# Score matmuls on 64-row tiles: heads of opposite parity share TensorE, one staged load, the weight splits and some GpSimd jobs move

## Chip, cores and metric

One NeuronCore of a Trainium2 chip. The metric is the device time of one execution in microseconds (us); each time shown is from the chip.

## What is computed

One block of a transformer on x of 4 batches x 512 tokens x 256, with modulation (adaLN), attention and a mixture of experts:

```python
mod = silu(c) @ wmod                      # six rows of 256 per batch: sa, ca, ga, sb, cb, gb
h = layernorm(x) * (1 + ca) + sa
q, k, v = split(h @ Wqkv.T + bqkv)        # 16 heads of 16
scores = q @ k.T * 16 ** -0.5             # causal: k > q becomes -inf
x = x + ga * (softmax(scores) @ v @ Wout.T + bout)
h = layernorm(x) * (1 + cb) + sb
x = x + gb * (shared_expert(h) + top_1_of_8_experts(h))   # silu(gate) * up, then down
```

The weights and activations that are multiplied are held as two 16-bit halves (high and low part), so that a product takes three matmuls.

## The kernel before

**Attention.** The tokens of a batch are four blocks of 128. The 16 heads of a batch form four groups of four heads; a group holds heads of one parity (`group_heads`: groups 0 and 2 even heads, 1 and 3 odd heads). For a pair of heads (even, odd) queries and keys stand one above the other in the stacks `qs` and `ks`, 48 rows (three 16-bit parts of 16 dimensions) from row 0 for the even head and 48 rows from row 64 for the odd one. `ks` holds ones elsewhere. `qs` of before has a copy for each parity with zeros in the other head's rows, so that a matmul over all rows sees one head. The last two rows of `qs` take the negated maxima of the rows, as high and low part.

The scores are computed twice. `scores(N)` (S, L1615) computes queries x keys, and a matmul (L1617) of the constant `maskb` with `identb` adds -1e30 above the diagonal; VectorE reduces the result to row maxima (`maxima`, L1137). `max_turn` transposes the maxima, VectorE negates them, SyncE writes them to `ng_d` (`maxima_out`, L559) and reads them back into `qs` (`maxima`, L566), for half the heads of a batch at a time. `scores_t(n)` (T, L1644) then computes the transposed scores with the maxima subtracted, ScalarE takes the exponential (`exps`, L887), GpSimd zeroes the masked triangle (`mask`, L759) and `values` (L1660, four 128x32 tiles side by side) multiplies with v. `turn_out` (L1670) transposes the result.

**The loop.** A batch is 44 steps, 11 for each group (`UNITS`). At step n of batch b each engine does T number 44 b + n, and S of number 44 b + n + 33 (`LAG`), that is three groups ahead: its heads have the opposite parity. The first 33 score units of batch 0 are computed in the head by another routine, `scores_apart`, on tiles of 32 rows (L1592). T writes two banks in turn (`t_bank`), S three others, so T of a step waits for the exponential of two steps earlier and S for the maximum of three steps earlier.

**Side jobs.** The table `SIDE` puts the other work (projections `qk` and `v`, transposes, output, statistics, modulation, router) at fixed steps; every engine walks the same steps, and `side_jobs(b, n)` gives it its part. On GpSimd `h_low` and `qk_low` (L733, L740) make low parts, `modulate2` (L766, L767) modulates, `bias_x` adds the bias, and `mask` stands at steps 3, 7, 9 and 10 of a group.

**Weights.** 27 pieces of the experts' weights are loaded (`stage_load` on SyncE for the first three, afterwards from ScalarE's queue), and split into halves during attention. `SPLITS` says at which step of which batch ScalarE makes the high half of piece k (`split_high`, L937); VectorE makes the low half two steps later (`LOWS`, L1238), and four steps later (`MOVES`) ScalarE waits for it and issues the write of the halves and the load of piece k + 3.

**The queue of SyncE** is written out by hand. In the head it issues for batches 0 and 1, for each half f of the heads, the writes of queries and keys to memory (`qk_out`, L532, six transfers), their reads into the stacks (`stacks`, L549, four), the maxima, the modulation rows (`mod_rows`, L555) and the first three staged loads. A wait in it holds up all that follows.

## Time and profile before

| what | us |
|---|---|
| runs shown: median, lowest, highest | 470.62, 469.96, 471.55 |
| the profiled execution | 467.88 |
| its span | 466.1 |
| TensorE busy | 401.6 (86%) |
| VectorE busy | 313.4 (67%) |
| ScalarE busy | 228.0 (49%) |
| GpSimd busy | 211.4 (45%) |
| mean granted clock of TensorE | 0.969 |

The span runs from the first to the last instruction that the profiler saw. PE is TensorE's matmuls, PEld its weight loads, DVE VectorE, ACT ScalarE, POOL GpSimd, SP SyncE; a q behind a name means the queue's sequencer, which waits or issues transfers. The ends of matmuls are modelled, so busy time of PE includes the way through the array. A granted clock of 1.00 is 2.4 GHz, 0.50 is 1.2 GHz.

### The profile page before, as it was taken

Reading aid. Unit: us, or ns where it says so; the run is one execution under the profiler, and the core shown is the slowest. Engines: PE = TensorE matmul, PEld = TensorE weight load, DVE = VectorE, ACT = ScalarE, POOL = GpSimd, SP = SyncE. Lnnn points to the kernel's source line nnn. Section 1 sums busy time; section 2 is a strip of 40 time slices with the busy share of each in tenths; the row PEclk is TensorE's granted clock in tenths of the full one; section 3 lists DMA queues with packets and bytes.
Section 4 is the critical chain, followed back from the end, with each engine's and each line's share of the span. In section 5 each row is a group of like instructions: output and inputs, shape, how many; then the busy total and the mean of one; then the engine's idle time right before and its main releaser. Section 6 shows DMA issues by size and latency. Waiting matters only on the chain.

```text
span 466.1 us, 8603 instructions
## 1 busy us (share of the span) xinstructions
PE 401.6 (86%) x3009; PEld 226.4 (49%) x3009; DVE 313.4 (67%) x635; ACT 228.0 (49%) x408; POOL 211.4 (45%) x251
## 2 busy tenths in 40 slices
PE   3789984889879879878988878999998999999991
PEld 3244532334544446433544345565655666666660
DVE  7678594359888878998887853789844444444441
ACT  2445663577574757736777545345222323232320
POOL 2395952543227934368252862110510646464332
PEclk9999998699999999997999979999999999999997
DMA  8456489268942588945446201995531454434210
GB/s 269 159 131 143 164 237 227 91 184 212 257 112 90 175 190 261 288 133 169 128 137 213 62 1 46 344 358 202 148 123 46 73 96 72 89 65 87 27 20 0
DMA packets 46192, 67.96 MB, mean 146 GB/s; under 512 B 5380, under 2 KB 33668, under 8 KB 46152
## 3 DMA queue, kind: packets, MB, share of 16 engines
q1 hardware_dynamic: 31064, 36.74, 27.8%
q10 hardware_dynamic: 9936, 22.55, 14.8%
q0 software_dynamic: 5152, 8.14, 8.9%
q8 instruction: 26, 0.43, 0.4%
q14 instruction: 14, 0.11, 0.1%
HBM read 43.14 MB, written 25.18 MB: 147 GB/s over the span
## 4 chain that ended last, share of the span: by engine, by line
PE 57%; DVE 16%; ACT 6%; POOL 6%; DMA 5%; issue 5%; SPq 3%; ACTq 1%; DVEq 0%; POOLq 0%
PE bank L1504 35%; PE bank L1660 5%; PE bank L1644 4%; DVE mx L1137 3%; PE bank L1615 3%; DMA stage<-in_down 2%; PE bank L1885 2%; DMA qk_d<-W 2%; ACT W L887 2%; PE bank L1592 1%; SPq L532 1%; DVE x_sb L1182 1%; DVE rowg L1238 1%; POOL W L740 1%; POOL W L759 1%
## 5 line engine op out<-in xcount | busy, mean ns | idle before, releaser
L887 ACT ACTIVATE W<-bank 128x512 f32<-128x512 f32 (+1 forms) x176 | 93.8, 562 | 63.5 <-PE bank L1644 42.4
L1137 DVE TENSOR_REDUCE mx<-bank 128x1 f32<-128x384 f32 (+3 forms) x176 | 105.2, 633 | 26.2 <-PE bank L1617 22.5
L1504 PE MATMUL bank<-W 128*128 128x256 f16 (+2 forms) x756 | 104.7, 291 | 4.5 <-DVE x_sb L1182 1.8
L1504 PEld LDWEIGHTS bank<-W 128*128 128x128 f16 x756 | 73.0, 99 | 37.8 <-issue 8.2
L759 POOL TENSOR_SCALAR_AFFINE_SELECT W<-W 128x512 f32<-128x512 f32 x64 | 48.7, 764 | 86.9 <-ACT W L887 86.8
L1644 PE MATMUL bank<-W 128*128 128x512 f16 (+3 forms) x256 | 64.1, 308 | 20.1 <-ACT W L887 18.8
L1504 PE MATMUL bank<-W,h2T 128*128 x276 | 67.3, 380 | 0.8 <-issue 0.8
L830 POOL DMA_INDIRECT out<-h2T,sidx x23 | 36.3, 1578 | 64.1 <-DVE h2T L1474 63.8
L1615 PE MATMUL bank<-W 126*128 126x128 f16 (+3 forms) x208 | 53.6, 309 | 5.2 <-DVE mx L1137 4.7
L1660 PE MATMUL bank<-W 128*32 128x128 f32 (+3 forms) x512 | 49.6, 462 | 4.5 <-POOL W L759 4.4
L1644 PEld LDWEIGHTS bank<-W 128*128 128x128 f16 x256 | 21.5, 98 | 58.5 <-ACT W L887 36.7
L1504 PE MATMUL bank<-h2T,W 128*128 128x512 f16 x192 | 43.1, 379 | 0.6 <-DVE W L1253 0.6
L1467 DVE TENSOR_TENSOR W<-bank,W 128x512 f16<-128x512 f32 x23 | 15.9, 692 | 37.4 <-ACT W L1048 37.4
L1048 ACT ACTIVATE W<-bank 128x512 f16<-128x512 f32 x23 | 13.7, 597 | 55.1 <-PE bank L1885 55.1
L1504 PEld LDWEIGHTS bank<-W,h2T 128*128 128x128 f16 x276 | 26.3, 97 | 26.3 <-issue 5.1
L816 POOL DMA_INDIRECT rowg<-h_d,gidx x23 | 23.6, 1028 | 31.4 <-DVE gidx L1417 24.7
L1617 PE MATMUL bank<-maskb,identb 128*128 128x128 bf16 (+2 forms) x143 | 35.7, 250 | 0.0
L1504 PEld LDWEIGHTS bank<-h2T,W 128*128 128x128 f16 x192 | 18.5, 98 | 21.9 <-DVE W L1253 1.0
L1238 DVE SCALAR_TENSOR_TENSOR rowg<-stage,rowg 128x1024 f16<-128x1024 f32 x18 | 23.3, 1293 | 7.6 <-ACT rowg L937 7.6
L876 ACT ACTIVATE W<-bank,bqk 128x512 f16<-128x512 f32 (+1 forms) x32 | 20.3, 685 | 15.8 <-PE bank L1504 15.6
L1615 PEld LDWEIGHTS bank<-W 126*128 126x128 f16 x208 | 19.5, 99 | 15.5 <-DVE mx L1137 7.7
L1269 DVE TENSOR_TENSOR h2T<-bank,h2T 128x256 f16<-128x256 f32 x23 | 9.8, 425 | 21.9 <-ACT h2T L916 21.9
(173 smaller groups left out, 557.3 us busy)
## 6 DMA issues: line engine op xcount, KB each, us to landing
w_d<-rowg ACTq DMA_DIRECT2D x18, 512.0 KB, 3.8
W<-w_d SPq DMA_DIRECT2D x18, 512.0 KB, 8.0
stage<-in_gup ACTq DMA_DIRECT2D x14, 512.0 KB
qk_d<-W SPq DMA_DIRECT2D x48, 128.0 KB
W<-qk_d SPq DMA_DIRECT2D x32, 192.0 KB, 5.5
stage<-in_down ACTq DMA_DIRECT2D x7, 512.0 KB
x_sb<-in_x SPq DMA_DIRECT2D x4, 512.0 KB, 8.9
h_d<-gbb SPq DMA_DIRECT2D x4, 512.0 KB, 4.6
```

Of the source, the lines that this page charges most:

```text
L759: g.affine_select(out=d, in_=d, compare_op=ALU.is_ge, fill=0.0, base=0, pattern=[[0, 4], [1, P]], channel_multiplier=-1).then_inc(s_msk, 1)
L816: g.indirect_dma_start(rowg[:, r % RG, :], None, h2_d, bass.IndirectOffsetOnAxis(ap=gidx[:, r:r + 1].bitcast(U32), axis=0)).then_inc(s_gr[ ...
L830: g.indirect_dma_start(out.rearrange("b s n -> (b s) n"), bass.IndirectOffsetOnAxis(ap=sidx[:, r:r + 1].bitcast(U32), axis=0), ry[r % YR], ...
L876: a.activation(dst, side_bank("qk", b, u)[:, :], ACT.Identity, bias=bqk[:, 2 * isk + u // 2:2 * isk + u // 2 + 1], scale=1.0 / WS if isk e ...
L887: a.activation(PT[j][:, i:i + m, :], t_bank(N)[:, 0:m * w].rearrange("p (i n) -> p i n", i=m), ACT.Exp).then_inc(s_exp, 1)
L1137: v.tensor_reduce(mx_v[:, b % 2, hp0 // 4, par, i:i + m, t], s_bank(N)[:, 0:m * w].rearrange("p (i n) -> p i n", i=m), AX.X, ALU.max).then ...
L1238: v.scalar_tensor_tensor(split_part(k, 1), staged(k), WS, split_part(k, 0), ALU.mult, ALU.subtract).then_inc(s_el, 1)
L1504: i = t_.matmul(outp, l, r, start=(n == 0), stop=(n == len(prods) - 1), **kw)
L1615: t_.matmul(bk[:, w * i:w * (i + 1)], qs[r][0:P - 2, hp, par, P * t:w], ks[r][0:P - 2, hp, 0:w], start=(i == 0), stop=False, skip_group_ch ...
L1617: t_.matmul(bk[:, 0:m * w].rearrange("p (i n) -> p i n", i=m)[:, :, w - P:w], identb[:, :], maskb[:, :].unsqueeze(1).to_broadcast([P, m, P ...
L1644: q = t_.matmul(t_bank(N)[:, w * i:w * (i + 1)], ks[r][:, hp, P * j:P * (j + 1)], qs[r][:, hp, par, P * j:S], start=True, stop=True)
L1660: q = t_.matmul(OTb[32 * i:32 * i + 32, P * j:S], v1[b % 2][:, c:c + 32], PT[j][:, i], start=(j == 0), stop=(j == TT - 1), tile_position=( ...
```

## The change

- **Tiles.** S and T use only the 64 rows of their head (48 rows of scores from row 0 or 64; T two more with the maxima). The maxima go to rows 48 and 49 of each half in place of rows 126 and 127, `qs` has one copy for both parities, and its two memsets of zeros (one on VectorE at the very start, one on GpSimd) go.
- **Mask.** The mask is added by two matmuls over the 64 rows of the same half, each for 64 of the 128 key columns, with new constants `half_q` and `half_m`, which GpSimd makes in the head (`half_constants`). TensorE waits for them once, before the first S.
- **Order in a group.** In steps 8 to 10 of a group T stands behind S.
- **Staged load.** `stage_load(2)` moves on SyncE from behind `mod_rows(0)` to behind `stacks(1, 0)`.
- **Splits.** `SPLITS` has 8, 6, 6 and 7 pieces in batches 0 to 3 in place of 6, 6, 8 and 7, at other steps.
- **GpSimd's jobs.** All but the two statistics and the bias stand two steps later in GpSimd's own order; the masks stay.

```diff
-          0: {6: 0, 12: 1, 18: 2, 25: 3, 32: 4, 39: 5},
-          1: {2: 6, 9: 7, 16: 8, 23: 9, 30: 10, 37: 11},
-          2: {1: 12, 6: 13, 11: 14, 16: 15, 21: 16, 26: 17, 31: 18, 36: 19},
+          0: {6: 0, 12: 1, 18: 2, 23: 3, 28: 4, 33: 5, 38: 6, 43: 7},
+          1: {5: 8, 12: 9, 19: 10, 26: 11, 33: 12, 40: 13},
+          2: {3: 14, 10: 15, 17: 16, 24: 17, 31: 18, 38: 19},
...
+def gpsimd_jobs(b, n):
+
+    if b < 0:
+        return side_jobs(b, n)
+    prompt = ("stats1", "stats2", "bias")
+    return ([j for j in side_jobs(b, n - 2) if j[0] not in prompt]
+            + [j for j in side_jobs(b, n) if j[0] in prompt])
...
+        half_q = sb("half_q", [P, 2, P], BF16)
+        half_m = sb("half_m", [P, P // 2], BF16)
...
-            qs.append(early(NH * S, F16).rearrange("p (h two n) -> p h two n", two=2, n=S))
+            qs.append(early(NH // 2 * S, F16).rearrange("p (h n) -> p h n", n=S))
+            at[0] += NH // 2 * S
...
-                    for a, dst in ((0, qs[r][:, :, par]), (1, ks[r])):
+                    for a, dst in ((0, qs[r]), (1, ks[r])):
...
-                    sp.dma_start(qs[r][P - 2:P, 4 * f:4 * f + 4, par], src[par]).then_inc(s_ng[r][f], 16)
+                    p0 = 64 * par + 3 * HD
+                    sp.dma_start(qs[r][p0:p0 + 2, 4 * f:4 * f + 4], src[par]).then_inc(s_ng[r][f], 16)
...
             stacks(1, 0)
+            stage_load(2)
             qk_out(1, 1)
             stacks(1, 1)
             sp.wait_ge(s_md, 16)
             mod_rows(0)
-            stage_load(2)
...
-                g.memset(qs[1].rearrange("p h two n -> p (h two n)").bitcast(F32), 0.0).then_inc(s_const, 1)
+                g.memset(ones16[:, :], 1.0).then_inc(s_const, 1)
                 po.wait_ge(s_const, 4)
-                g.memset(ones16[:, :], 1.0)
...
+            def half_constants():
+
+                link(g.memset(half_q[:, :, :], 0.0))
+                for lo in (0, P // 2):
+                    rows = slice(lo, lo + P // 2)
+                    link(g.memset(half_m[rows, :], 0.0))
+                    link(g.affine_select(out=half_m[rows, :], in_=half_m[rows, :], compare_op=ALU.is_ge, fill=NEG,
+                                         base=0, pattern=[[-1, P // 2]], channel_multiplier=1))
+                    link(g.affine_select(out=half_m[rows, :], in_=half_m[rows, :], compare_op=ALU.not_equal, fill=NEG,
+                                         base=-(P // 2 - 1), pattern=[[0, P // 2]], channel_multiplier=1))
+                    for part, half in ((0, 0), (1, 0), (1, 1)):
+                        sel = half_q[rows, part, 64 * half:64 * half + 64]
+                        link(g.affine_select(out=sel, in_=sel, compare_op=ALU.not_equal, fill=1.0,
+                                             base=0, pattern=[[-1, P // 2]], channel_multiplier=1))
+                    for part, half, value in ((0, 0, 0.0), (1, 0, 1.0), (1, 1, 0.0)):
+                        sel = half_q[rows, part, 64 * half:64 * half + 64]
+                        link(g.affine_select(out=sel, in_=sel, compare_op=ALU.not_equal, fill=value,
+                                             base=-(P // 2 - 1), pattern=[[0, P // 2]], channel_multiplier=1))
+                g.tensor_copy(ve1[0:1, 0:1], ve1[0:1, 0:1]).then_inc(s_half, 1)
+                po.wait_ge(s_half, 1)
...
-                    for job, c, k in side_jobs(b, n):
+                    for job, c, k in gpsimd_jobs(b, n):
...
-            v.memset(qs[0].rearrange("p h two n -> p (h two n)").bitcast(F32), 0.0)
...
+                if N == LAG:
+                    pe.wait_ge(s_half, 1)
...
-                    t_.matmul(bk[:, w * i:w * (i + 1)], qs[r][0:P - 2, hp, par, P * t:w],
-                              ks[r][0:P - 2, hp, 0:w], start=(i == 0), stop=False, skip_group_check=True)
-                t_.matmul(bk[:, 0:m * w].rearrange("p (i n) -> p i n", i=m)[:, :, w - P:w], identb[:, :],
-                          maskb[:, :].unsqueeze(1).to_broadcast([P, m, P]), start=False, stop=True,
-                          skip_group_check=True).then_inc(s_s1, 1)
+                    p0 = 64 * par
+                    t_.matmul(bk[:, w * i:w * (i + 1)], qs[r][p0:p0 + 3 * HD, hp, P * t:w],
+                              ks[r][p0:p0 + 3 * HD, hp, 0:w], start=(i == 0), stop=False, skip_group_check=True)
+                rows = slice(64 * par, 64 * par + 64)
+                for part in range(2):
+                    c = w - P + 64 * part
+                    q = t_.matmul(bk[:, 0:m * w].rearrange("p (i n) -> p i n", i=m)[:, :, c:c + 64],
+                                  half_q[rows, part, :], half_m[rows, :].unsqueeze(1).to_broadcast([64, m, 64]),
+                                  start=False, stop=(part == 1), skip_group_check=True)
+                q.then_inc(s_s1, 1)
...
-                    q = t_.matmul(t_bank(N)[:, w * i:w * (i + 1)], ks[r][:, hp, P * j:P * (j + 1)],
-                                  qs[r][:, hp, par, P * j:S], start=True, stop=True)
+                    rows = slice(64 * par, 64 * par + 3 * HD + 2)
+                    q = t_.matmul(t_bank(N)[:, w * i:w * (i + 1)], ks[r][rows, hp, P * j:P * (j + 1)],
+                                  qs[r][rows, hp, P * j:S], start=True, stop=True)
...
-                    if b >= 0:
+                    if b >= 0 and n % UNITS < 8:
...
+                    if b >= 0 and n % UNITS >= 8:
+                        scores_t(BU * b + n)
```

TensorE, batch 0, steps 7 to 9 of its second group, before (L1644 is T, L1615 S, L1617 the mask, L1660 `values`):

```order
L1615 MATMUL bank<-W 128x512
L1617 MATMUL bank<-maskb,identb 128x128
L1644 MATMUL bank<-W 128x256 x2
L1615 MATMUL bank<-W 128x512
L1617 MATMUL bank<-maskb,identb 128x128
L1660 MATMUL bank<-W 32x512 x4
L1644 MATMUL bank<-W 128x256 x2
L1615 MATMUL bank<-W 128x512
L1617 MATMUL bank<-maskb,identb 128x128
```

and after (L1683 is T, L1649 S, L1654 the mask's two matmuls, L1699 `values`):

```order
L1649 MATMUL bank<-W 128x512
L1654 MATMUL bank<-half_m,half_q 128x64 x2
L1649 MATMUL bank<-W 128x512
L1654 MATMUL bank<-half_m,half_q 128x64 x2
L1683 MATMUL bank<-W 128x256 x2
L1699 MATMUL bank<-W 32x512 x4
L1649 MATMUL bank<-W 128x512
L1654 MATMUL bank<-half_m,half_q 128x64 x2
L1683 MATMUL bank<-W 128x256 x2
L1649 MATMUL bank<-W 128x512
```

From step 8 on T has moved behind S and the mask, and stands next to `values`; the mask is two matmuls.

SyncE, in the head, from the stacks of batch 1's first half, before (L549 `stacks`, L532 `qk_out`, L555 `mod_rows`, L501 the staged load, L559 and L566 the maxima of batch 0's second half):

```order
L549 DMA W<-qk_d 48x4x512 x4
L532 DMA qk_d<-W 8x16x512 x6
L549 DMA W<-qk_d 48x4x512 x4
L555 DMA W<-mod_d 128x768
L501 DMA stage<-in_down 128x4x256
L559 DMA ng_d<-negm 32x2x128
L566 DMA W<-ng_d 2x4x512 x2
```

and after (L559 `stacks`, L514 the staged load, L545 `qk_out`, L565 `mod_rows`, L569 and L577 the maxima):

```order
L559 DMA W<-qk_d 48x4x512 x4
L514 DMA stage<-in_down 128x4x256
L545 DMA qk_d<-W 8x16x512 x6
L559 DMA W<-qk_d 48x4x512 x4
L565 DMA W<-mod_d 128x768
L569 DMA ng_d<-negm 32x2x128
L577 DMA W<-ng_d 2x2048 x2
```

The staged load has moved ahead of six writes, four reads and the modulation rows.

ScalarE, batch 2, around step 22, before (L887 exponentials of steps 21 to 26, L937 the high half of a split, L941, L494 and L495 its move and the load behind it):

```order
L887 ACTIVATE W<-bank 128x512
L937 ACTIVATE rowg<-stage 128x1024
L887 ACTIVATE W<-bank 128x512 x4
L941 DMA w_d<-rowg 128x2048
L494 DMA stage<-in_sgw 128x512
L495 DMA stage<-in_suw 128x512
L887 ACTIVATE W<-bank 128x384
```

and after (L919 exponentials, L969 high half, L973, L507 and L508 move and load, L927 the copy that was L895):

```order
L969 ACTIVATE rowg<-stage 128x1024
L919 ACTIVATE W<-bank 128x384
L919 ACTIVATE W<-bank 128x512 x3
L973 DMA w_d<-rowg 128x2048
L507 DMA stage<-in_sgw 128x512
L508 DMA stage<-in_suw 128x512
L919 ACTIVATE W<-bank 128x512 x3
L969 ACTIVATE rowg<-stage 128x1024
L919 ACTIVATE W<-bank 128x512
L919 ACTIVATE W<-bank 128x384
```

Before, the split of step 21 is moved four exponentials later, at step 25. After, the splits stand at steps 17 and 24 and the first one's move at step 21.

## Rows read from the trace of the kernel before

**Rows 1.** Busy time of the engines by stretch: length, then each engine; clock, transfers.

```profile
53.80:86.30 32.50, 21.77 (x165) 10.96 (x165) 22.06 (x47) 17.14 (x31) 15.94 (x19) 0.88 0.71 187
86.30:114.90 28.60, 25.86 (x190) 11.85 (x189) 18.48 (x32) 19.56 (x35) 12.43 (x17) 0.95 0.66 182
114.90:175.80 60.90, 51.32 (x437) 27.29 (x436) 51.64 (x104) 39.06 (x71) 30.70 (x39) 1.00 0.61 168
175.80:230.10 54.30, 48.00 (x410) 25.07 (x408) 49.22 (x96) 34.76 (x62) 28.19 (x38) 0.94 0.68 207
230.10:288.60 58.50, 50.40 (x395) 25.57 (x394) 41.83 (x77) 36.92 (x68) 28.34 (x35) 0.94 0.30 92
70.00:80.00 10.00, 4.85 (x37) 2.58 (x35) 5.24 (x10) 4.10 (x8) 2.91 (x3) 0.94 1.05 258
```

**Rows 2.** Chain that ended last, shares by line, windows 86:115, 115:176, 176:230.

```profile
by line: PE bank L1660 18.9%; PE bank L1504 18.9%; PE bank L1644 17.3%; PE bank L1615 14.1%; PE bank L1617 6.7%; PE bank L1670 4.0%; DVE rowg L1238 3.9%; ACT rowg L937 3.3%; ACT W L887 3.1%; issue 3.0%; ACT W L876 2.4%; ACTq L499 1.6%; ACTq
by line: DVE mx L1137 7.5%; POOL W L740 7.4%; PE bank L1504 7.0%; DVE rowg L1238 6.2%; POOL rowg L766 6.2%; issue 5.8%; POOL W L759 5.6%; POOL rowg L767 5.1%; DVE x_sb L1182 4.1%; PE bank L1660 3.8%; ACT W L887 3.7%; ACTq L501 3.4%; PE bank
by line: PE bank L1660 15.8%; PE bank L1644 14.2%; PE bank L1504 11.4%; PE bank L1615 10.2%; issue 6.3%; ACT W L887 5.0%; DVE x_sb L1182 4.6%; PE bank L1617 4.1%; ACT rowg L937 3.0%; DVE rowg L1180 2.9%; DVE st L1187 2.4%; PE bank L1670 2.4
```

**Rows 3.** Timeline of SyncE's queue: start, us, engine, line, transfer.

```profile
59.62 3.66 SPq L532 DMA_DIRECT2D qk_d<-W  x6
...
70.65 0.47 SPq L501 DMA_DIRECT2D stage<-in_down  x1
71.16 0.48 SPq L559 DMA_DIRECT2D ng_d<-negm  x1
82.28 0.55 SPq L566 DMA_DIRECT2D W<-ng_d  x2
```

**Rows 4.** Timeline, ScalarE and TensorE, the stall; idle before in brackets.

```profile
81.57 1.06 ACT L937 ACTIVATE rowg<-stage 128x1024 f16<-128x1024 f32 x1 [7.12 <-DMA stage<-in_down]
...
83.17 0.61 PE L1644 MATMUL bank<-W 128*128 128x128 f16 x4 [7.99 <-ACT W L887]
```

**Rows 5.** Timeline of TensorE in the head: 32-row tiles, whole-array matmuls.

```profile
41.92 0.82 PE L1592 MATMUL bank<-W 32*128 32x512 f16 x12
...
42.80 1.46 PE L1504 MATMUL bank<-W 128*128 128x512 f16 x6
...
49.80 2.76 PE L1504 MATMUL bank<-W 128*128 128x512 f16 x12
```

**Rows 6.** Timeline of TensorE: what follows a mask matmul of 128 columns.

```profile
40.61 0.23 PE L1585 MATMUL bank<-maskb,identb 128*128 128x128 bf16 x1
...
40.77 0.34 PE L1592 MATMUL bank<-W 32*128 32x128 f16 x3
...
60.41 0.22 PE L1617 MATMUL bank<-maskb,identb 128*128 128x128 bf16 x1
...
60.55 1.06 PE L1660 MATMUL bank<-W 128*32 128x512 f32 x8
...
62.00 0.22 PE L1617 MATMUL bank<-maskb,identb 128*128 128x128 bf16 x1
...
62.06 0.38 PE L1644 MATMUL bank<-W 128*128 128x128 f16 x4
```

**Rows 7.** Timeline, VectorE's and GpSimd's memsets, GpSimd's idle time in the head.

```profile
1.71 3.47 DVE L1304 MEMSET W<- 128x4096 f32 x1 [1.71 <-PEq L1942]
...
29.77 3.51 POOL L683 MEMSET W<- 128x4096 f32 x1
...
40.17 1.15 POOL L733 TENSOR_TENSOR W<-W 128x512 f16<-128x512 f32 x1 [4.24 <-ACT W L862]
```

**Rows 8.** Timeline of TensorE in batch 1: `values` behind a mask.

```profile
165.59 0.42 PE L1660 MATMUL bank<-W 128*32 128x128 f32 x8 [1.36 <-POOL W L759]
```

**Rows 9.** Timeline in batch 2: VectorE's half of a split, ScalarE idle.

```profile
207.35 1.22 DVE L1238 SCALAR_TENSOR_TENSOR rowg<-stage,rowg 128x1024 f16<-128x1024 f32 x1
...
210.35 0.49 ACT L887 ACTIVATE W<-bank 128x384 f32<-128x384 f32 x1 [4.91 <-issue]
```

More of the change, by code:

```diff
@@ L317, in build @@
         s_col = sem("s_col")
-        s_zero = sem("s_zero")
+        s_ones = sem("s_ones")
+        s_half = sem("s_half")
         s_mp = sem("s_mp")
@@ L537, in stacks @@
                 sp.wait_ge(s_qkw[r][f], 16 * 6 * (b // 2 + 1))
-                if b == 0 and f == 0:
-                    sp.wait_ge(s_zero, 1)
-                if b == 1 and f == 0:
-                    sp.wait_ge(s_const, 4)
-                    sp.wait_ge(s_zero, 2)
+                if b < 2 and f == 0:
+                    sp.wait_ge(s_ones, b + 1)
                 if b >= 2:
@@ L787, in _ @@
                         more_constants()
+                        half_constants()
                     if b < 0 and n in (25, 38):
@@ L1307, in _ @@
             norm1(0)
-            v.memset(ks[0].rearrange("p h n -> p (h n)").bitcast(F32), ONES).then_inc(s_zero, 1)
+            v.memset(ks[0].rearrange("p h n -> p (h n)").bitcast(F32), ONES).then_inc(s_ones, 1)
             modulation_columns()
             low_qkv()
-            v.memset(ks[1].rearrange("p h n -> p (h n)").bitcast(F32), ONES).then_inc(s_zero, 1)
+            v.memset(ks[1].rearrange("p h n -> p (h n)").bitcast(F32), ONES).then_inc(s_ones, 1)
             stats1(1)
```

## The prediction

> **What bounds the kernel now.** I read the page first, then the busy time of each stage, then the chain of waits, and last the timeline at the places where the chain changes engine. The attention loop (52 to 289 us) is cut by batch, batch 0 again at 86.3 us [rows 1]. TensorE is busy for 25.9 of 28.6 us late in batch 0, 51.3 of 60.9 in batch 1, 48.0 of 54.3 in batch 2; VectorE for 51.6 and 49.2 us in batches 1 and 2. So no engine alone sets the pace. The chain of waits says who does where [rows 2]. Late in batch 0 the two score passes and the mask (L1644, L1615, L1617) hold 38.1% of 29 us, 11.0 us; in batch 2 28.5% of 54 us, 15.4 us; in batch 1 they are not among the first names and GpSimd's lines (L740, L766, L759, L767) hold 24.3% of 61 us. After 289 us the kernel is not touched.
>
> **Early batch 0, a long stall.** SyncE issues the third staged load at 70.65 us, behind both parts of batch 1's stacks [rows 3]. ScalarE reaches the weight split that reads it, gets it at 81.57, and TensorE, two exponentials behind, starts again at 83.17 after 8.0 us idle [rows 4]. That idle time also costs clock: 0.88 of full speed granted over this stage [rows 1].
>
> **What the change costs and saves, on TensorE.** A matmul of 512 columns takes 0.217 us of TensorE: twelve in 2.76 against six in 1.46 [rows 5]. On 32-row tiles, in the same place, twelve take 0.82: four run side by side [rows 5]. A group of 11 steps has 5120 columns in each score pass and 2048 in the mask, 12288 or 5.2 us. In the new order T (`scores_t`) and S (`scores`) of a step read opposite halves of the array and write different banks, so for steps 0 to 7 a step costs the longer of both: 5 x 512 + 3 x 384 = 3712 columns. In steps 8 to 10, S comes first; T of step 9 runs beside S of step 10, T of 8 and 10 are alone because `values` follows: 5 x 512. With the mask's 2048, which the 64-column halves do not change (4 x 64 twice is 4 x 128), 8320 columns are left, 3.5 us; if the second mask half runs beside the next T, some 0.3 less. I take 1.8 us saved per group, 35%. There are 13 such groups (143 units of S): 23 us of TensorE's time.
>
> Against this, every change of tile shape costs. Same shape: the mask at 62.00 is followed at 62.06. Other shape: mask at 60.41, `values` at 60.55; mask at 40.61, 32-row tiles at 40.77 [rows 6]. That is 0.09 to 0.10 us more. Counted in the two orders of instructions, the loop has 132 changes of shape before and 226 after (by batch 29, 34, 34, 35, then 48, 62, 54, 62), because each projection, transpose or shared matmul now stands between 64-row tiles. 94 x 0.095 = 8.9 us. If TensorE had to run empty at each, a switch would cost what a 128-column matmul lasts beyond its columns, 0.22 - 0.055 = 0.165 us, and 94 of them 15.5 us; the rows show the smaller price. The Trainium skill ("TensorEngine Tiling (Array Packing)", Key Properties) has a rule that speaks against the change: a change of the tiling mode, not of the tile, drains the engine; by it the second sum would stand, by the rows the first, and I take the first.
>
> **By stage, on the path.**
> - Head: VectorE's memset of `qs[0]`, 3.47 us, opens the chain [rows 7]. It goes, but the input's landing and TensorE's first matmuls, which wait for the modulation weights, are close behind: -0.4 (0 to -1.5). GpSimd loses a memset of 3.51 us and gets 19 small linked operations and a copy, at 0.25 to 0.36 us each some 5 to 7 us; it has 4.24 us idle before 40.17 [rows 7], so 4.24 + 3.51 covers it. Without that cover it would be late by up to 1 us: then batch 1's low parts and modulation rows, and SyncE's stacks behind them, are late.
> - Early batch 0: the load is now issued at about 59.6 us, before `qk_out(1, 1)`, 11 us earlier, and lands before 71. The 8.0 us don't come back whole. Next late is step 22, which needs the maxima of the second half of the heads: written from 71.16, read back from 82.28 [rows 3]. The transfer engines are busy all of the time from 70 to 80 us, share 1.05 [rows 1], and they drain in order of issue; the bytes ahead of that write are the same, only earlier. `qk_out(1, 1)` is issued 0.5 us later and lands up to 2 us later, the stacks behind it too. I let the maxima land 1 to 3.5 us earlier: -2.5 (0 to -8).
> - Late batch 0: 35% of 11.0 is -3.9; nine or ten switches, four fifths on the path, +0.7; two more splits (a copy of 1.06 us on ScalarE [rows 4] and a pass of 1.22 on VectorE [rows 9] each), some of it in idle time, +1.5. Sum -1.7.
> - Batch 1: T, S and mask on the path, perhaps 3 us: -1.0. GpSimd: its masks are queued behind modulation and low-part jobs; TensorE waits 1.36 us for one at 165.59 [rows 8]. Two steps later for the jobs puts those masks ahead of about 2.7 us of work: -1.9. One more VectorE split spilling in: +0.5. Sum -2.4 (+1 to -7; VectorE's 51.6 + 1.2 us are the floor).
> - Batch 2: 35% of 15.4 is -5.4, switches 20 x 0.095 x 0.6 = +1.2. Two splits fewer, -1. And ScalarE sits idle for 4.91 us before 210.35, stuck at the move of the split of step 21: VectorE's half of it is queued behind the second statistics and starts at 207.35 [rows 9], the exponentials wait behind the move, clock 0.94 in the stage [rows 1]. The splits move to steps 17 and 24, away from step 22: -2 to -4. Together -7 to -9, but VectorE's 49.2 - 2.5 = 46.7 us leave at most 7.6: I take -6.
> - Batch 3: one group has S left (-1.8), 27 more switches +2.6; two fifths on the path: +0.3.
>
> Sum: -0.4 - 2.5 - 1.7 - 2.4 - 6.0 + 0.3 = -12.7. The profiled execution took 467.88 us, the median of the runs is 470.62, 2.7 above; 470.6 - 12.7 = 457.9.
>
> **Rivals.**
> 1. *VectorE, GpSimd and the maxima end it.* The time that TensorE saves turns into waits for VectorE, as in batch 1, where TensorE holds little of the chain [rows 2]. Then stages give 0, -1, -0.5, -1, -2.5: -5, 465.6 us. For: busy shares of 85% and 91%. Against: 15.4 us of plain score matmuls on the path of batch 2.
> 2. *Slower: no overlap.* If T and S don't run side by side (each waits for another engine's semaphore before it, and a waiting T holds up the S behind it), nothing of the 23 us comes, and the switches remain: 8.9 us, of which at the path's shares about 5.5; with mask halves that no longer hide, +1. The stall, the stats collision and the memset return some 5 to 6. That is +1; with each switch at 0.165 us (94 x 0.165 x 0.6 = 9.3 in place of 5.5) +5, 475. This second price is what the skill's rule above would give. The rival decides as soon as fewer than about a quarter of the pairs overlap. Against it: the 32-row tiles of this trace do overlap [rows 5].
> 3. *Clock.* Three times in the loop TensorE fell to 1.2 GHz after waits (shares 0.88, 0.95, 0.94, 0.94 [rows 1]); each time cost some 7 to 10 us at half speed. A TensorE with less to do may fall more often; two more drops of 7 us cost +7: about 465.
> 4. *More.* The stall comes back whole and VectorE closes up: -20, 450.
> 5. *The parts hardly act:* overlap and switches cancel, the stall only moves: within 0.3% (1.4 us, about what a measurement of this kernel can tell from no change).
>
> **How the numbers follow.** Forecast 0.60, with its own range 453 to 463.5; rivals 1 and 3 together 0.20; slower 0.08; more 0.07; none 0.05. Leaving out the slow end and a part of "more" and "none" gives 450 to 467.5. Faster by over 0.3%: 0.60 + 0.07 + 0.20 = 0.87; within: 0.05; slower: 0.08.
>
> **What would show it.** Right: in the timeline T and S starting within 0.01 us of each other; late batch 0 and batch 2 shorter by 2 and 6 us; no idle time of 8 us before 84 but one of some 5 to 6 us at step 22, ended by a transfer; shape changes still 0.15 us from a 128-column matmul. Wrong: S starting 0.2 us behind T; new stretches at 1.2 GHz; GpSimd busy without a break up to 41 us with SyncE's mod rows late; VectorE busy over 95% in batch 1.

## The result, and the profile after

The changed kernel took 476.27 us (median of 4, 470.52 to 477.04), beside it the kernel before 470.29: ratio 1.0097, 95% interval 1.0052 to 1.0141. Later, on another chip, it took 472.41 against 469.80, ratio 1.0030 (0.9990 to 1.0070). So it is 0.3 to 1% slower by the two measurements, and the second can't be told from no change; I had said 458. (A ratio leaves out executions more than 1.5% above their kernel's fastest; a median takes all.)

Busy time by stretch in the profiled execution (476.57 us, span 474.8), cut at the same exponentials as [rows 1], columns as there; the last row is the part behind the loop:

```profile
53.80:86.90 33.10, 21.82 (x188) 11.93 (x189) 22.99 (x47) 17.33 (x31) 17.19 (x20) 0.77 0.72 185
86.90:118.50 31.60, 27.30 (x210) 11.11 (x206) 19.49 (x32) 21.52 (x38) 11.84 (x16) 0.81 0.74 216
118.50:176.60 58.10, 49.72 (x485) 26.00 (x482) 50.33 (x104) 39.34 (x70) 31.99 (x40) 0.94 0.63 178
176.60:233.10 56.50, 48.19 (x451) 24.73 (x449) 48.28 (x93) 31.83 (x59) 26.46 (x36) 0.85 0.54 160
233.10:292.10 59.00, 54.12 (x409) 25.40 (x409) 43.05 (x80) 37.36 (x69) 28.97 (x36) 0.91 0.32 99
292.10:474.70 182.60, 165.38 (x1114) 105.71 (x1106) 91.43 (x205) 56.22 (x107) 63.20 (x53) 0.98 0.42 112
```

Against [rows 1]: +0.6, +3.0, -2.8, +2.2, +0.5 us. The eighth column tells most: the granted clock is lower in every stretch of the loop, 0.77, 0.81, 0.94, 0.85, 0.91 where it was 0.88, 0.95, 1.00, 0.94, 0.94. TensorE's busy time over the five stretches rose from 197.4 to 201.2 us although its matmuls overlap, as more of them ran at half speed. In the loop of this execution TensorE stood at 1.2 GHz ten times, 61 us together; before, three times and 24 us. Counting time at 1.2 GHz as 2 x (1 - clock) x time, it is 69 us of a whole execution in the mean of the four; before, at a mean clock of 0.967, 31 us.

The overlap itself is there. Timeline of TensorE in the kernel after: start, us, line, tile:

```profile
180.21 0.33 PE L1683 MATMUL bank<-W 50*128 50x384 f16 x1
180.21 0.33 PE L1649 MATMUL bank<-W 48*128 48x384 f16 x1
180.38 0.22 PE L1654 MATMUL bank<-half_m,half_q 64*128 64x64 bf16 x2
180.53 0.68 PE L1535 MATMUL bank<-W 128*128 128x256 f16 x4
```

T (L1683) and S (L1649) start together (3 or 4 ns apart in most records where T is issued first, 10 ns in most where S is), and the mask follows 0.17 us later, the time of one pass. By an estimate that sums what each matmul's columns occupy at 2.4 GHz, a group of 11 steps went from 9.5, 11.5, 11.0, 8.3 us (first, sixth, ninth, thirteenth group) to 7.2, 9.7, 9.2, 6.5: 1.8 to 2.3 us, the 1.8 of the forecast. In the records the next shape starts 0.12 us behind the last mask half, which has 64 columns (0.03 us), so a change of shape costs 0.09 as in [rows 6].

Early batch 0 with its stall came out no shorter. SyncE's queue, then TensorE, in the kernel after:

```profile
60.76 0.48 SPq L514 DMA_DIRECT2D stage<-in_down  x1
61.28 4.37 SPq L545 DMA_DIRECT2D qk_d<-W  x6
73.59 2.03 SPq L559 DMA_DIRECT2D W<-qk_d  x4
...
76.15 0.43 SPq L569 DMA_DIRECT2D ng_d<-negm  x1
84.39 0.53 SPq L577 DMA_DIRECT2D W<-ng_d  x2
```

```profile
65.90 0.50 PE L1649 MATMUL bank<-W 48*128 48x128 f16 x3 [2.31 <-DMA W<-qk_d]
...
86.30 0.60 PE L1683 MATMUL bank<-W 50*128 50x512 f16 x1 [6.53 <-DMA W<-ng_d]
```

The chain of waits from 86 to 119 us, in which TensorE's score and mask lines held 38.1% before [rows 2], is now led by the transfers:

```profile
by line: DMA ng_d<-negm 21.5%; DMA qk_d<-W 16.6%; DMA W<-ng_d 15.9%; SPq L545 11.1%; PE bank L1535 8.1%; issue 6.3%; SPq L559 4.6%; PE bank L1699 4.1%; PE bank L1649 3.4%; ACT rowg L969 3.2%; ACT W L908 3.0%; PE bank L1683 2.6%; PE bank L16
```

The load stands 10 us earlier (60.76), but `qk_out(1, 1)` behind it took until 73.59 to land, so the stacks are issued 5.8 us later than before (67.82), the maxima are written at 76.15 instead of 71.16, and their read is issued at 84.39 instead of 82.28 [rows 3]. The 8.0 us of [rows 4] became 6.53, ended by the maxima, and the wait for batch 1's stacks grew from 0.5 to 2.31 us. The load's move also explains the chain from 86 to 119 us: e1 below, which has the move and whole-array tiles, is led there by the same transfers (22.6%, 18.2% and 13.2% of 86 to 116 us), and e7, which has not, by TensorE's lines.

### The profile page after: what moved, and what is told of

It reads as the page before. It is cut to its first block, busy times and chain, and to the rows that moved or that the text cites. A ratio compares the mean times of both kernels' runs of the same rounds, so it can differ in the third digit from the quotient of the medians.

```text
span 474.8 us, 8919 instructions
## 1 busy us (share of the span) xinstructions
PE 407.1 (86%) x3152; PEld 225.9 (48%) x3152; DVE 311.3 (66%) x634; ACT 227.9 (48%) x408; POOL 212.9 (45%) x270
## 4 chain that ended last, share of the span: by engine, by line
PE 53%; DVE 15%; DMA 11%; ACT 7%; issue 5%; SPq 4%; POOL 4%; ACTq 1%; DVEq 0%; POOLq 0%
PE bank L1535 35%; DMA ng_d<-negm 4%; DMA qk_d<-W 4%; DVE mx L1169 4%; PE bank L1699 4%; PE bank L1683 2%; SPq L545 2%; PE bank L1926 2%; DVE rowg L1270 2%; ACT W L919 2%; PE bank L1623 1%; DMA stage<-in_wmod 1%; POOL W L790 1%; PE bank L1649 1%; PE bank L1550 1%
## 5 line engine op out<-in xcount | busy, mean ns | idle before, releaser
L919 ACT ACTIVATE W<-bank 128x512 f32<-128x512 f32 (+1 forms) x176 | 93.6, 562 | 72.0 <-PE bank L1683 49.8
L1535 PE MATMUL bank<-W 128*128 128x256 f16 (+2 forms) x756 | 109.2, 298 | 6.7 <-DVE x_sb L1214 2.9
L1535 PEld LDWEIGHTS bank<-W 128*128 128x128 f16 x756 | 73.9, 101 | 42.6 <-issue 11.6
L1683 PE MATMUL bank<-W 50*128 50x512 f16 (+3 forms) x256 | 65.1, 330 | 19.1 <-ACT W L919 9.9
L1535 PE MATMUL bank<-W,h2T 128*128 x276 | 68.6, 386 | 3.2 <-DVE W L1285 2.0
L1649 PE MATMUL bank<-W 48*128 48x128 f16 (+3 forms) x208 | 57.0, 336 | 8.9 <-DVE mx L1169 6.5
L1699 PE MATMUL bank<-W 128*32 128x128 f32 (+3 forms) x512 | 54.3, 501 | 0.7 <-POOL W L790 0.7
L1683 PEld LDWEIGHTS bank<-W 50*128 50x128 f16 x256 | 18.5, 96 | 53.2 <-ACT W L919 23.1
L1080 ACT ACTIVATE W<-bank 128x512 f16<-128x512 f32 x23 | 13.7, 597 | 55.6 <-PE bank L1926 53.2
L1498 DVE TENSOR_TENSOR W<-bank,W 128x512 f16<-128x512 f32 x23 | 15.9, 692 | 37.4 <-ACT W L1080 37.4
L1654 PE MATMUL bank<-half_m,half_q 64*128 64x64 bf16 (+2 forms) x286 | 38.5, 217 | 0.0
L1654 PEld LDWEIGHTS bank<-half_m,half_q 64*128 64x128 bf16 x286 | 28.8, 105 | 12.3 <-issue 4.6
L1649 PEld LDWEIGHTS bank<-W 48*128 48x128 f16 x208 | 17.0, 99 | 28.5 <-DVE mx L1169 16.1
```

Of the source, the lines that this page charges most:

```text
L919: a.activation(PT[j][:, i:i + m, :], t_bank(N)[:, 0:m * w].rearrange("p (i n) -> p i n", i=m), ACT.Exp).then_inc(s_exp, 1)
L1498: v.tensor_tensor(rhT[:, r % 2, 1].rearrange("p f n -> p (f n)"), T1[:, :], rhT[:, r % 2, 0].rearrange("p f n -> p (f n)"), ALU.subtract). ...
L1535: i = t_.matmul(outp, l, r, start=(n == 0), stop=(n == len(prods) - 1), **kw)
L1649: t_.matmul(bk[:, w * i:w * (i + 1)], qs[r][p0:p0 + 3 * HD, hp, P * t:w], ks[r][p0:p0 + 3 * HD, hp, 0:w], start=(i == 0), stop=False, skip ...
L1654: q = t_.matmul(bk[:, 0:m * w].rearrange("p (i n) -> p i n", i=m)[:, :, c:c + 64], half_q[rows, part, :], half_m[rows, :].unsqueeze(1).to_ ...
L1683: q = t_.matmul(t_bank(N)[:, w * i:w * (i + 1)], ks[r][rows, hp, P * j:P * (j + 1)], qs[r][rows, hp, P * j:S], start=True, stop=True)
```

## The experiments

Sixteen kernels, four at a time, each four on one chip with the kernel before. The clock is the mean over a kernel's executions; before had 0.967 to 0.969 each time.

| kernel | median us | before | ratio (95%) | clock |
|---|---|---|---|---|
| e1 three moves, tiles as before | 462.14 | 467.29 | 0.9893 (0.9840-0.9947) | 0.977 |
| e2 tiles only | 473.71 | 467.29 | 1.0118 (1.0062-1.0175) | 0.926 |
| e3 changed, load back | 469.70 | 467.29 | 1.0021 (0.9983-1.0060) | 0.930 |
| e4 changed, T twice in even steps | 472.10 | 467.29 | 1.0073 (1.0035-1.0111) | 0.939 |
| e5 changed + 64 filler matmuls | 473.96 | 467.30 | 1.0147 (1.0093-1.0200) | 0.945 |
| e6 e1 + the same filler | 465.71 | 467.30 | 0.9984 (0.9949-1.0019) | 0.982 |
| e7 splits and GpSimd, load as before | 459.67 | 467.30 | 0.9852 (0.9807-0.9898) | 0.976 |
| e8 e1, load behind the maxima | 459.98 | 467.30 | 0.9851 (0.9807-0.9894) | 0.977 |
| e9 changed, T and S in one half | 500.68 | 467.12 | 1.072 (of medians; its shortest execution, 487.40, 1.043) | 0.871 |
| e10 changed, transfers as e8 | 467.84 | 467.12 | 1.0009 (0.9977-1.0040) | 0.927 |
| e11 GpSimd's jobs only | 467.87 | 467.12 | 1.0025 (0.9991-1.0059) | 0.972 |
| e12 changed, T first | 469.73 | 467.12 | 1.0013 (0.9976-1.0050) | 0.928 |
| e13 splits only | 468.80 | 469.80 | 0.9952 (0.9924-0.9980) | 0.974 |
| e14 e7, score matmuls on 66 rows | 474.05 | 469.80 | 0.9930 (0.9890-0.9969) | 0.943 |
| e15 e10, T first | 470.66 | 469.80 | 1.0018 (0.9987-1.0049) | 0.928 |
| e16 changed, again | 472.41 | 469.80 | 1.0030 (0.9990-1.0070) | 0.929 |

**Tiles or moves (e1, e2, e3).** Two theories stood against each other: "clock" (the tiles lower it) and "load" (the moved load holds up the transfers behind it). e1 is before with the new table, `gpsimd_jobs` and this; e2 is the reverse, the changed kernel with the three as before; e3 undoes this line alone:

```diff
             stacks(1, 0)
+            stage_load(2)
             qk_out(1, 1)
             stacks(1, 1)
...
             mod_rows(0)
-            stage_load(2)
```

> The kernel before, with only the three moves of the change: the third staged load ahead of qk_out(1, 1), the new table of splits, GpSimd's jobs two steps later. The score tiles stay whole-array. Theory 'load': the moved load holds up what is issued behind it, so batch 1's stacks land later (TensorE waits about 2 us for them near 66 us instead of 0.47), the maxima of step 22 are written out at about 76 us instead of 71.16, and the stall before 86 us stays; the GpSimd wait of 4.4 us shrinks; sum 0 to +3 us against before, 470 to 473. Theory 'clock': the moves have little to do with the loss, the time at 1.2 GHz stays near the 31 us of before, and the kernel stands within 2 us of before. My forecast of record would have had the moves alone at -5 to -7, 464.

> The changed kernel with the staged load, the table of splits and GpSimd's jobs as before, so only the 64-row tiles, the halved mask and the step order are new. Theory 'clock': TensorE has less to do, falls to 1.2 GHz more often (60 us or more at that level against 31), and the saving of the overlap is lost: 468 to 476. Theory 'load': the loss of the changed kernel sits in the moved load, so the tiles alone bring what the forecast gave them (batches 0, 1 and 2: about -8 us): 461 to 464, with the clock of before.

> The changed kernel with the third staged load back behind mod_rows(0). Theory 'load': the stacks land by 64 to 66 us, the maxima are written out at 71 us, batch 1's first exponential starts 3 us earlier than in the changed kernel, and one or two stretches at 1.2 GHz before 130 us go with the waits: 3 to 6 us faster than the changed kernel, 471 to 473. Theory 'clock': the drops after 150 us stay as they are, and it gains at most 2 us: 474 to 476.

The moves alone gain 5.2 us, the tiles alone lose 6.4 (medians), at a clock of 0.926: the loss is the tiles'. In e1 the maxima were written at 74.27 us and the stall was 7.76 us, so the theory on the load was right in its mechanism; but e1 is faster all the same, which neither theory had, and which is the splits' and GpSimd's doing (e7). e3, with the load back, stands at 1.0021, against 1.0097 in the first measurement of the changed kernel, which seemed to bear out the theory on the load; but the changed kernel run again stands at 1.0030 (e16). With the tiles in place, undoing this move brings nothing that shows. e3's twelve executions differ among themselves: 464.58 us at a clock of 0.939, 473.90 at 0.918. A straight line through them gives 0.47 us for each us at 1.2 GHz; through the 23 executions of before beside them 0.59. The Trainium skill ("TensorE: Matmul & The Clock Gate", Terms, `throttle_active_nc0_time_ns`) prices throttled time at a half at this ratio; these two slopes lie on either side of it. The same line through each of the sixteen kernels gives anything from 0.22 to 0.68, 0.43 in the mean, so a half is a fair first price here and no more.

**Does more work raise the clock? (e4, e5, e6)**

```diff
-                for i in range(m):
+                for i in [i for i in range(m) for _ in range(2 - N % 2)]:
```

```diff
+                if N % UNITS in (0, 2, 4, 7):
+                    t_.matmul(t_bank(N)[:, 0:4 * P], identb[:, :], maskb[:, :].unsqueeze(1).to_broadcast([P, 4, P]),
+                              start=True, stop=True)
```

> The changed kernel with the matmuls of T issued twice in every even step (the second writes the same values again): 88 steps, about 41,000 more columns of 64-row tiles, 17 us of TensorE at 2.4 GHz, which brings its score work near that of the kernel before. Theory 'clock': the fuller TensorE falls to 1.2 GHz less often, the time there shrinks from 70 us by a third or more, and the kernel is no more than 4 us slower than the changed one, perhaps faster. If the clock doesn't follow TensorE's load, two thirds of the 17 us are on the path: +10 us or more, 486.

> The changed kernel with one useless whole-array matmul of 512 columns (0.217 us) ahead of T in 4 steps of each group of 11, 64 in all, where TensorE changes its tile shape anyway; T then overwrites what it wrote. 14 us more of TensorE, and some 5 us for 48 more changes of shape. Theory 'clock' (TensorE's level follows how much of the array is at work, and the tiles lowered that): the mean granted clock rises from 0.93 towards the 0.97 of the kernel before, and the time stays within 3 us of the changed kernel or falls below it. If the level doesn't answer to it, 19 us more on TensorE give +8 to +12 us, 482 or more, at 0.93.

> The same 64 useless matmuls at the same places in the kernel with whole-array score tiles and the three moves (the first experiment, 462.1 us, clock 0.978). Here the clock has little left to give, so this shows the plain price of that work: 14 us of TensorE and few changes of shape, about half of it on the path: +5 to +9 us, 467 to 471, by both theories. If it costs as much as in the changed kernel, the clock gave nothing back there.

T twice lifted the clock from 0.929 to 0.939, from 67 us at 1.2 GHz to 58, not by the third that I expected; whole-array filler of fewer columns lifted it to 0.945, 52 us. In time neither gave anything back that shows: e4 (1.0073) is level with the changed kernel (1.0030 and 1.0097), e5 (1.0147) is 0.5 to 1.2% slower, and the same filler in whole-array tiles cost 0.9% (0.9893 to 0.9984), less than the 5 to 9 us that I expected. The clock moves with TensorE's load, but too little to say what it answers to.

**Busy time or rows at work (e9, e14).** e9 moves T to the rows of the other parity: the same matmuls, waits and shapes, no overlap. e14 leaves tiles alone: in e7's kernel both passes read 66 rows of operands, still whole-array matmuls in the same order (the diff shows S; T gets the same `0:66`). Both change the values as well: e9's T computes the scores of the wrong heads, and e14 leaves out nearly all of the odd heads' scores and all maxima.

```diff
-                    rows = slice(64 * par, 64 * par + 3 * HD + 2)
+                    rows = slice(64 * (1 - par), 64 * (1 - par) + 3 * HD + 2)
```

```diff
-                    t_.matmul(bk[:, w * i:w * (i + 1)], qs[r][0:P - 2, hp, par, P * t:w],
-                              ks[r][0:P - 2, hp, 0:w], start=(i == 0), stop=False, skip_group_check=True)
+                    t_.matmul(bk[:, w * i:w * (i + 1)], qs[r][0:66, hp, par, P * t:w],
+                              ks[r][0:66, hp, 0:w], start=(i == 0), stop=False, skip_group_check=True)
```

> The changed kernel, but T reads the rows of the other parity, so T and S of a step use the same half of the array and can't run side by side. T then computes the scores of the wrong heads: this part of the output is not the reference's, the work and its waits are the same. It takes back the whole 23 us of TensorE that the overlap saves and keeps every change of shape. If the clock follows how much of the time TensorE is busy, the mean granted clock goes from 0.927 back to 0.95 or more, and the time moves by -2 to +5 us against the changed kernel (474 to 481). If the clock follows how much of the array is at work (one half at a time here, as little as can be), it stays at 0.93 or falls, and the kernel is 10 us or more slower, 486.

> The seventh experiment's kernel (whole-array score tiles, 459.7 us, clock 0.976), but both score passes read 66 rows of operands in place of 126 and 128, so the matmuls, their columns, their order and their tile shape stay the same and only fewer rows of the array are at work. Half of the heads' scores and the maxima that stand in the other rows are left out of the sums, so the output is not the reference's. If the granted clock follows the rows at work, it falls with no tile or order changed: to 0.95 or less, and the time rises by some 0.5 us for each microsecond at 1.2 GHz, to 464 to 470. If the clock fell in the changed kernel because of idle time, waits or shape changes, it stays at 0.975 and 460.

In e9 the clock fell to 0.871: 129 us at 1.2 GHz. The profiled execution is the longest of the six (503.67 us, clock 0.859); the shortest, 487.40 us, had 0.899, still below every execution of the changed kernel. The first row shows a stretch of e9; the other two show T and S at another place at 1.2 GHz, 0.43 us apart and no longer together:

```profile
227.00:281.60 54.60, 54.32 (x291) 23.53 (x292) 34.03 (x58) 24.91 (x44) 17.94 (x25) 0.50 0.23 76
```

```profile
190.87 0.63 PE L1683 MATMUL bank<-W 50*128 50x512 f16 x1
191.30 0.52 PE L1649 MATMUL bank<-W 48*128 48x384 f16 x1
```

TensorE was busy for 54.32 of 54.60 us and got 0.50 of full speed all that time. So it isn't idle time that keeps the clock down here. The fall itself came behind idle time: in the 5 us before 227.0 TensorE was busy for 3.02. The Trainium skill ("TensorE: Matmul & The Clock Gate", Part 1: The HAM clock gate) has the clock set by how busy the engine has been; this stretch, busy throughout and at 1.2 GHz, differs from that, and the measurement decides. e14 lowers the clock without tiles, more changes of shape or a new order. Batch 2 of e14 in windows:

```profile
174.10:208.60 34.50, 30.12 (x261) 16.69 (x258) 30.16 (x62) 21.16 (x39) 14.61 (x23) 1.00 0.74 205
208.60:229.10 20.50, 19.71 (x94) 9.11 (x94) 13.61 (x25) 9.66 (x17) 9.01 (x13) 0.50 0.31 98
```

and the same windows of e7, whose matmuls differ in the rows that they read alone:

```profile
170.80:205.00 34.20, 29.88 (x260) 16.54 (x258) 30.34 (x63) 21.05 (x39) 14.79 (x23) 1.00 0.69 203
205.00:222.70 17.70, 15.31 (x148) 7.35 (x145) 16.82 (x30) 10.43 (x20) 11.84 (x14) 1.00 0.34 114
```

The batch's 23rd exponential comes 28.3 us after its first in e14 and 28.2 in e7, the 34th 43.2 and 40.2. In between TensorE falls to 1.2 GHz for 20.5 us, where e7, doing the same work, stays at 2.4. It isn't that e14 was idle more: in the 5 us before 208.6 TensorE was busy for 3.29, and in the 5 us before 205.0 in e7 for 3.29 too. Over 14 executions e14's mean clock is 0.943 (0.908 to 0.965), e7's 0.976 over 6 (0.968 to 0.982), and by medians against before e14 is 1.009 where e7 was 0.984; 474.05 us lies above the top of my 464 to 470.

The difference doesn't rest on the long executions: e14's five shortest (465.46 to 468.17 us) had clocks of 0.957 to 0.965, e7's five shortest (459.12 to 461.39) 0.975 to 0.982, and the ratios of the table are 0.9930 and 0.9852. The two kernels ran on different chips, but e13, on e14's, had 0.974. So reading fewer rows of operands lowered the clock, with order, columns and shapes unchanged. Whether it goes by the rows at work or by the values in them e14 alone can't say, since its values changed too. In the pair e8 and e10 below the scores are the same and, beside the halved mask, only rows of zeros go; the clock falls there too, with the tiles as the other difference.

**The price of the tiles in a better order of transfers (e8, e10).** Both take the load out of the way of step 22's maxima (shown below), and move batch 0's splits from the third on to steps 24, 28, 32, 36, 40 and 43:

```diff
                 maxima_out(b, 1)
                 maxima(b, 1)
+                if b == 0:
+                    stage_load(2)
```

> The first experiment's kernel with the third staged load issued behind the maxima's write and read of step 22 in place of ahead of them, and batch 0's splits from the third on at steps 24, 28, 32, 36, 40, 43. If the transfers issued ahead of that write are what makes the stall before 85 us, the write lands by about 76 us and not at 82.5, the stall shrinks from 7.8 to 1 to 3 us, and the kernel comes to 457 to 460. If the stall has another cause (the stacks, VectorE's maxima, a later split that ScalarE waits for), it stays near 462.

> The changed kernel with the order of transfers of the eighth experiment (third staged load behind the maxima of step 22, batch 0's later splits at steps 24 to 43), which brought that kernel to 460. If the tiles themselves are the loss (clock), the pair differs by the tiles alone and this one is 8 to 12 us slower than 460: 468 to 472 at a clock of 0.93. If the tiles only lost because they met late transfers in batch 0, it comes to 455 to 461 at 0.96 or more.

e8's SyncE queue and TensorE:

```profile
70.66 0.51 SPq L568 DMA_DIRECT2D ng_d<-negm  x1
78.17 0.70 SPq L575 DMA_DIRECT2D W<-ng_d  x2
```

```profile
80.33 0.39 PE L1654 MATMUL bank<-W 128*128 128x512 f16 x1 [4.55 <-DMA W<-ng_d]
```

The maxima come 4.1 us earlier than before (78.17 against 82.28) and the stall is 4.55 us; my 76 us and 1 to 3 were too good. Yet e8 is no faster than e7. In the profiled executions the second group of batch 0 (the eleven steps before step 22) took 15.3 us in place of e7's 20.3, but the fourth took 15.0 in place of 10.9 and batch 1 as a whole 58.6 in place of 55.8. e10 differs from e8 by the tiles alone, with their mask halves and the order in steps 8 to 10: +7.9 us, clock 0.927 against 0.977, 68 us at 1.2 GHz against 21. That is the cleanest price of the tiles, 1.6%; e15 against e8, with T first in all steps, gives 1.7%. In the profiled executions batch 0 takes 60.8 us in both, though the clock fell there too (0.84 against 0.95); batches 1, 2 and 3 take 60.9, 57.0 and 58.8 us in e10 (clock 0.86, 0.81, 0.91) and 58.6, 53.2 and 55.8 in e8 (0.96, 1.00, 0.97). So what a microsecond at 1.2 GHz costs depends on the stage.

**Which of the moves (e7, e11, e13).** e7 has both the table and `gpsimd_jobs`, e11 only the latter, e13 only the table.

> The kernel before with the new table of splits and GpSimd's jobs two steps later; the staged load stays behind mod_rows(0). In the first experiment the moved load delayed batch 1's stacks and the maxima of step 22 (written at 74.27 us), and the stall before 85 us was still 7.8 us. Theory 'the load's move is worth nothing or harms': 460 to 462, no slower than the first experiment. Theory 'the load's move brought the gain': the time goes back to 465 to 467.

> The kernel before with GpSimd's jobs two steps later and nothing else. My forecast gave this part -1.9 us in batch 1, and gave the splits -2 to -4 in batch 2. The two together measured -7.6 us. If GpSimd's part is as forecast, 464.5 to 466, and the splits are the larger part; if the waits for GpSimd's masks cost more than the 1.36 us that I read at one place, 460 to 463.

> The kernel before with the new table of splits and nothing else. GpSimd's later jobs alone measured no difference (467.9), both together -7.6 us. If the two add up, the splits alone give all of it: 459 to 461. If they need each other (the splits free TensorE and ScalarE, and then GpSimd's masks are late), 462 to 465.

Neither alone does much (-0.5% and +0.2%), together -1.5%: they need each other. `values` on TensorE from 86 to 289 us, first e13, then e7; behind the last bar its idle time and what ended it:

```profile
L1660 PE MATMUL bank<-W 128*32 128x384 f32 (+3 forms) x472 | 44.8, 454 | 6.5 <-POOL W L759 6.5
```

```profile
L1669 PE MATMUL bank<-W 128*32 128x256 f32 (+3 forms) x464 | 43.7, 451 | 0.8 <-POOL W L768 0.8
```

In the kernel before the same wait is 4.2 us. With the splits out of the way the kernel runs ahead and waits for GpSimd's masks instead (6.5); with the jobs two steps later that wait is gone (0.8). The load's move, the third part, brings nothing and may cost: e1 has it and e7 not, 462.14 against 459.67 on two chips, ratios 0.9893 and 0.9852 with intervals that overlap. In the profiled executions batch 0 took 63.2 us in e1 and 61.1 in e7, as before the change.

**The step order, and the end of the kernel (e12, e15, e16).**

```diff
-                    if b >= 0 and n % UNITS < 8:
+                    if b >= 0:
                         scores_t(BU * b + n)
...
-                    if b >= 0 and n % UNITS >= 8:
-                        scores_t(BU * b + n)
```

> The changed kernel with T ahead of S in all steps, as before the change, so in steps 8 to 10 too. T and S of these steps then still run side by side. If the swap helps (VectorE gets its maxima earlier), this is 1 to 3 us slower than the changed kernel, 476 to 479; if late T holds up ScalarE's exponentials of those steps, it is 1 to 3 us faster, 472 to 474. The clock stays near 0.93 by both.

> The tenth experiment's kernel (64-row tiles, transfers in the better order, 467.8 us) with T ahead of S in all steps. The order of T and S in steps 8 to 10 measured 0.8% in the changed kernel (1.0013 against 1.0097), if that is the order's and not the difference between two sessions. If it is the order's: 463 to 465. If not: 467 to 468. Either way not below the 460 of the same schedule with whole-array tiles, as long as the clock stays near 0.93.

> The changed kernel once more, unedited, beside the others on the same chip. Its profiled execution lost 5.3 us more than before in the part after the loop, which the change doesn't touch and which all later kernels, with tiles or without, did at the old length. If that is an accident of those executions, it now stands at 1.003 to 1.007 of before (469 to 471), and the order of T and S is worth little; if it belongs to this kernel, it comes to 1.01 again with the longer end.

T first makes no difference that these runs can tell (e12 against e16, e15 against e10, all within 0.2%). The part behind the loop took 182.6 us in the profile after and 177.3 before; the profiled executions of the tile kernels from e2 to e12 came to within 3 us of before there. On the chip of e13 to e16 all four, e13 without tiles too, were 3 us or more longer there. So the 5.3 us are not the tiles', and part of the first measurement's 1% is likely chance, which isn't shown; what VectorE waits for there ("issue", 2.85 us before 344.84 us) I did not find out.

## Why the prediction was wrong

**The sum kept the clock of before; that step failed.** "35% of 11.0 is -3.9", "35% of 15.4 is -5.4" and the rest price saved columns at 2.4 GHz. The columns went as computed (1.8 us a group), the shape changes cost what I took (0.095 us), T and S overlapped. But the tiles took TensorE to 1.2 GHz for some 38 to 48 us more, which at half a microsecond for each is 19 to 24 us, an estimate, against forecast tile terms of -8.1 us (-3.9 + 0.7, -1.0, -5.4 + 1.2, +0.3). Net that would be +11 to +16; e8 and e10 measure +7.9, so either the overlap brought more than 8 or a microsecond at 1.2 GHz costs less than half, as the slope of 0.29 in e4 and 0.23 in e10 suggests. Which, these runs don't settle.

**Rival 3 had the mechanism and the wrong size.** "Two more drops of 7 us cost +7: about 465" became five to seven more drops (eight to ten in the loops of the kernels with overlapping tiles, three before) and some 40 us. Its reason, "a TensorE with less to do may fall more often", was at most half of it: more work did lift the clock a little (e4, e5), but e9 had more to do than the changed kernel and stayed at 1.2 GHz longest. By e14 and e10, the rows of zeros that the whole-array score tiles multiplied, useless to the result, seem to have helped to keep the clock up. [rows 1] had shown 0.88 to 0.95 in three of the four stretches before 230 us; a kernel so near the edge should have given that rival the largest chance, not a share of 0.20.

**Early batch 0, -2.5, came out +0.6.** "The bytes ahead of that write are the same, only earlier" failed: I took `qk_out(1, 1)` to land "up to 2 us later"; the stacks behind it were issued 5.8 later and the maxima written 5.0 later. The order that shortens this stall is the reverse (e8).

**Late batch 0, -1.7, came out +3.0:** clock 0.81, and at 118.0 us a new wait of 2.13 us for the next maxima. Most of it is the load's move and not the tiles': with whole-array tiles the same stretch took 31.2 us in e1, which has the move, and 28.4 in e7, which has not, against 28.6 before. TensorE's score lines were no longer on the path there, so the -3.9 for them had little to shorten. This is rival 1 in one stage: transfers and maxima ended it. **Batch 1, -2.4, came out -2.8**, and the match is luck. The sum left out batch 1's 28 additional changes of shape, 2.7 us of TensorE, though it counted them; and without tiles the stage took 55.8 us in e7 and 58.9 in e1 in place of 60.9: the moves alone gave 5.1 and 2.0. The -1.9 for GpSimd rested on one wait of 1.36 us; e11 shows that the part is worth nothing alone; on top of the splits it adds about 1% (0.9952 to 0.9852). **Batch 2, -6, came out +2.2:** the collision before 210 us in [rows 9] is gone (e7 does the third group in 12.0 us in place of 15.9), but the other groups grew, and the batch took 52.5 us in e7 and 53.0 in e13 in place of 54.3: -1.8 and -1.3, where the splits' share was -3 to -5. The tiles' share of -4.2 was lost at a clock of 0.85. **Head, -0.4:** first exponential at 53.8 both times, 0; GpSimd's small operations fitted into its idle time, with 1.25 us left before 40.21. **Batch 3, +0.3, came out +0.5,** by luck again: in e7 it took 56.1 us in place of 58.5 without tiles, and the tiles took it back. (All these lengths are of one profiled execution each.)

**Rival 2, slower for want of overlap,** had the sign and the wrong reason; e9 shows what that case really costs, 500 us (487 in its shortest execution) and not 475, and the clock goes with it. Rivals 4 and 5 didn't occur, rival 1 only late in batch 0.

## What to carry to other kernels

Before packing small matmuls side by side in a kernel that already drops to 1.2 GHz, price the clock first: read a stretch with fewer rows of operands, as e14 did, and see what it does to the granted clock. That takes one edit and no new tiles. Measure a change's parts alone and together; here a gain of 1.5% (e7, the fastest kernel of this study with e8) was hidden under a loss of 1.6%, two moves worth nothing or little alone were worth 7.6 us together, and two stages came out as forecast only because two errors cancelled. A transfer moved ahead in a queue is paid for by all that stand behind it: count when those land, not only the one moved.

## What the hardware showed

- TensorE busy for 54.32 of 54.60 us at 0.50 of full speed (e9), with matmuls that read 48 and 50 rows in one half of the array, the mask and `values` between them.
- The same matmuls on 66 rows in place of 126 and 128: mean clock 0.943 in place of 0.976, and more scatter between executions (465.46 to 490.52 us). The values changed with the rows.
- Two passes on 64-row tiles in opposite halves start 3 or 4 ns apart in most records with T first, 10 ns with S first; in the same half, 0.43 us apart at 1.2 GHz, which is the 512 columns of the first.
